# Summing the gate over partitions on VectorE instead of TensorE, in an expert MLP kernel

## What is computed

```python
x = x + (einsum('bsd,bdh->bsh', x, W[cat]) + b[cat])     # layer 0; B=2, S=1024, D=256
# layer 1, on that x:
s0   = relu(x @ swi[0]) @ swo[0]                         # shared expert 0, F=1024
s1   = relu(x @ swi[1]) @ swo[1]                         # shared expert 1
eo   = relu(x @ wi[type]) @ wo[type]                     # the chosen expert of each batch
gate_in = concatenate([eo[:, 0], s0[:, 0], s1[:, 0]])    # first token only: 3 x 256 numbers per batch
w    = softmax(relu(gate_in @ g1) @ g2)                  # g1: 768 x 256, g2: 256 x 3
out  = x + eo * w[0] + s0 * w[1] + s1 * w[2]
```

## Time and profile before

| | |
|---|---|
| median of 3 runs | 271.71 us (271.42 to 271.82) |
| the profiled execution's own time | 271.66 us |
| its span (first to last instruction) | 269.8 us |
| TensorE busy | 265.1 us, 98% of the span |
| VectorE, ScalarE, GpSimd busy | 160.9, 148.2, 160.8 us (55 to 60%) |
| granted TensorE clock | 0.999 of full |

### The profile page before, as it was taken

One profiled execution on the slowest core, in us unless ns is written; L12 is line 12 of the kernel. 1 busy time (PEld: TensorE's weight loads), 2 busy tenths in 40 slices (PEclk: granted clock), 3 DMA queues, 4 the chain that ended last, 5 costly groups with the idle time before them and its releaser, 6 DMA issues.

```text
span 269.8 us, 3491 instructions
## 1 busy us (share of the span) xinstructions
PE 265.1 (98%) x1182; PEld 220.3 (82%) x1182; DVE 160.9 (60%) x241; ACT 148.2 (55%) x257; POOL 160.8 (60%) x170
## 2 busy tenths in 40 slices
PE   8999999999999999999999999999999999999994
PEld 8788887888888888888888888888888888888884
DVE  3879958635644444654445565345566477685684
ACT  2597357665565655665655653745644555645320
POOL 0179989999948949938944724724725528524000
PEclk9999999999999999999999999999999999999999
DMA  6735322022012022102022112112012022000008
GB/s 193 247 106 155 117 78 79 7 75 79 6 74 78 6 73 78 58 24 78 2 78 78 34 46 78 33 46 79 19 61 78 2 78 75 2 0 2 0 12 299
DMA packets 7328, 18.30 MB, mean 68 GB/s; under 512 B 1168, under 2 KB 1936, under 8 KB 7312
## 3 DMA queue, kind: packets, MB, share of 16 engines
q1 hardware_dynamic: 6592, 16.92, 18.4%
q10 hardware_dynamic: 720, 1.18, 1.4%
HBM read 16.00 MB, written 2.10 MB: 67 GB/s over the span
## 4 chain that ended last, share of the span: by engine, by line
PE 96%; DMA 2%; SPq 1%; DVE 0%; issue 0%; ACT 0%; DVEq 0%
PE acc L657 48%; PE chain L657 24%; PE right L657 12%; PE left L657 7%; PE acc L674 4%; DMA w_raw<-cat_w 2%; PE corner L657 1%; SPq L222 1%; PE left L813 0%; DVE x L648 0%; ACT w_hi L352 0%; PE left L819 0%; SPq L224 0%; DVEq L647 0%
## 5 line engine op out<-in xcount | busy, mean ns | idle before, releaser
L264 POOL TENSOR_TENSOR m_lo<-staged,m_hi 128x512 fp32r<-128x512 f32 (+1 forms) x48 | 81.5, 1706 | 80.5 <-ACT m_hi L340 65.7
L657 PE MATMUL acc<-h_hi,m_hi 128*128 128x512 f32 x190 | 73.9, 389 | 0.0
L657 PE MATMUL acc<-h_hi,m_lo 128*128 128x512 f32 x190 | 73.9, 389 | 0.0
L657 PE MATMUL acc<-h_lo,m_hi 128*128 128x512 f32 x190 | 73.9, 389 | 0.0
L364 ACT COPY kept<-chain 128x512 f32<-128x512 f32 x66 | 38.8, 588 | 57.8 <-PE chain L657 57.8
L657 PEld LDWEIGHTS acc<-h_hi,m_lo 128*128 128x128 f32 x190 | 35.7, 188 | 7.4
L657 PEld LDWEIGHTS acc<-h_hi,m_hi 128*128 128x128 f32 x190 | 35.7, 188 | 7.4
L657 PEld LDWEIGHTS acc<-h_lo,m_hi 128*128 128x128 f32 x190 | 35.7, 188 | 7.4
L471 DVE SCALAR_TENSOR_TENSOR h_lo<-left,h_hi 128x512 fp32r<-128x512 f32 x24 | 16.6, 692 | 29.9 <-ACT h_hi L376 29.9
L264 POOL TENSOR_TENSOR staged<-staged 128x128 f32<-128x128 f32 x66 | 30.9, 482 | 1.7
L476 DVE TENSOR_TENSOR left<-left,kept 128x512 f32<-128x512 f32 x22 | 15.3, 698 | 26.7 <-PE left L657 26.7
(11 more groups left out here) (107 smaller groups left out, 442.7 us busy)
## 6 DMA issues: line engine op xcount, KB each, us to landing
staged<-mlp_w SPq DMA_DIRECT2D x22, 512.0 KB, 3.3
x<-x_t ACTq DMA_DIRECT2D x4, 256.0 KB, 3.9
staged<-mlp_w SPq DMA_DIRECT2D x4, 256.0 KB, 3.3
x<-x_t SPq DMA_DIRECT2D x4, 256.0 KB, 5.4
out_t<-x SPq DMA_DIRECT2D x2, 512.0 KB, 3.3
g_sb<-g SPq DMA_DIRECT2D x1, 768.0 KB, 3.8
out_t<-x SPq DMA_DIRECT2D x3, 256.0 KB, 3.0
w_raw<-cat_w SPq DMA_DIRECT2D x4, 128.0 KB, 3.1
```

The costliest lines, as they stand in the source:

```text
L264: return nc.gpsimd.tensor_tensor(out, a, b, ALU.subtract)
L657: last = nc.tensor.matmul(out[:, columns], half[:, slot, at:at + P], moving[:, columns], start=(start and n == 0), stop=(stop and n == 2), ...
```

## The change

The sum over the partitions of `gate_part` moves from TensorE to VectorE. The 128x512 tile is transposed in blocks of 32x32; the 32 numbers of each row of a block are then summed, which leaves 16 partial sums on each partition (partition 32 i + c holds those of quarter i, for the features that are c modulo 32). Four copies bring the four quarters side by side on partitions 0 to 31, a second row sum adds them, and relu, the product with `g2` and a row sum over 8 features per logit follow on 32 partitions. The last matmul then sums over 32 partitions instead of 128. `g2` is loaded in another layout, by two DMAs instead of one, and `PAD` grows from 40 to 152.

```diff
-PAD = 40
+PAD = 152
-        g2_sb = sb("g2_sb", [P, DC, 3])
+        g2_sb = sb("g2_sb", [SQ, DC, P // SQ, 3])          # SQ = 32
-        gate_h = sb("gate_h", [P, B * DC])
-        logit_half = sb("logit_half", [P, B, 3])
-        logit_part = sb("logit_part", [P, B, 3])
+        gate_blocks = sb("gate_blocks", [P, B * D])
+        gate_quarter = sb("gate_quarter", [P, B * D // SQ])
+        gate_all = sb("gate_all", [SQ, P // SQ, B * D // SQ])
+        gate_h = sb("gate_h", [SQ, B * D // SQ])
+        logit_terms = sb("logit_terms", [SQ, B, 3, D // SQ])
+        logit_part = sb("logit_part", [SQ, B, 3])
...
-                    sp.dma_start(g2_sb[:], g2).then_inc(g_loaded, 16)
+                    for d in range(DC):
+                        sp.dma_start(g2_sb[:, d, :, :], g2[:, d, :].rearrange("(a c) k -> c a k", c=SQ)).then_inc(g_loaded, 16)
...
+            def gate_transpose():
+
+                dve.wait_ge(gate_sums, 12)
+                nc.vector.transpose(gate_blocks[:], gate_part[:].rearrange("p b n -> p (b n)")).then_inc(gate_steps, 1)
+
+            def gate_quarters():
+                dve.wait_ge(gate_steps, 1)
+                nc.vector.tensor_reduce(gate_quarter[:], gate_blocks[:].rearrange("p (n k) -> p n k", k=SQ), AX.X, ALU.add
+                                        ).then_inc(gate_steps, 1)
+
             def gate_logits():
-                dve.wait_ge(gate_hidden_done, 1)
-                nc.vector.tensor_scalar(gate_h[:], left[:, 0:B * DC], 0.0, None, ALU.max).then_inc(gate_steps, 1)
-                dve.wait_ge(gate_steps, 1)
+                dve.wait_ge(gate_steps, 2)
+                for i in range(P // SQ):
+                    nc.vector.tensor_copy(gate_all[:, i, :], gate_quarter[i * SQ:(i + 1) * SQ, :]).then_inc(gate_steps, 1)
+                dve.wait_ge(gate_steps, 2 + P // SQ)
+                nc.vector.tensor_reduce(gate_h[:], gate_all[:].rearrange("c i n -> c n i"), AX.X, ALU.add).then_inc(gate_steps, 1)
+                dve.wait_ge(gate_steps, 3 + P // SQ)
                 for b in range(B):
...
+                    h = gate_h[:, b * (D // SQ):(b + 1) * (D // SQ)].unsqueeze(1).to_broadcast([SQ, 3, D // SQ])
+                    nc.vector.scalar_tensor_tensor(out=logit_terms[:, b, :, :], in0=h, scalar=0.0,
+                                                   in1=g2_sb[:].rearrange("c d a k -> c k (d a)"),
+                                                   op0=ALU.max, op1=ALU.mult).then_inc(gate_steps, 1)
+                dve.wait_ge(gate_steps, 3 + P // SQ + B)
+                nc.vector.tensor_reduce(logit_part[:], logit_terms[:], AX.X, ALU.add).then_inc(gate_steps, 1)
...
                 hidden_lo(j, 0)
+                if j == KEPT * GROUPS + 2:
+                    gate_transpose()
+                if j == KEPT * GROUPS + 3:
+                    gate_logits()
...
                 if j == KEPT * GROUPS + 2:
-                    gate_logits()
+                    gate_quarters()
...
-                if j == KEPT * GROUPS + 2:
+                if j == KEPT * GROUPS + 3:
 
                     pe.wait_ge(h_split, 4 * j + NTH[0])
-                    pe.wait_ge(gate_sums, 12)
-                    for b in range(B):
-                        for d in range(DC):
-                            last = nc.tensor.matmul(left[:, b * DC + d:b * DC + d + 1], gate_part[:, b, d * P:(d + 1) * P],
-                                                    ones[:, 0:1], start=True, stop=True)
-                    last.then_inc(gate_hidden_done, 1)
-                if j == KEPT * GROUPS + 3:
-                    pe.wait_ge(h_split, 4 * j + NTH[0])
-                    pe.wait_ge(gate_steps, 1 + 2 * B)
-                    nc.tensor.matmul(left[:, 8:8 + B * 3], ones[:], logit_part[:].rearrange("p b k -> p (b k)"),
+                    pe.wait_ge(gate_steps, 4 + P // SQ + B)
+                    nc.tensor.matmul(left[:, 8:8 + B * 3], ones[0:SQ, :], logit_part[:].rearrange("p b k -> p (b k)"),
                                      start=True, stop=True).then_inc(logits_done, 1)
```

More of the change, by code:

```diff
@@ L20 @@
 SLOTS = 3
+SQ = 32
 RAW_A21, RAW_S = 896, 1024
@@ L148, in build @@
         gate_sums = sem("gate_sums")
-        gate_hidden_done = sem("gate_hidden_done")
         gate_steps = sem("gate_steps")
@@ L490, in gate_partial @@
                         if kind == 0 and d == 0:
-                            dve.wait_ge(g_loaded, 32)
+                            dve.wait_ge(g_loaded, 16 * (1 + DC))
                             nc.vector.tensor_scalar(gate_part[:, b, :], row, first_token, None, ALU.mult).then_inc(gate_sums, 1)
@@ L500, in _ @@
             gate_count = [0]
-            def gate_logits():
-                dve.wait_ge(gate_hidden_done, 1)
-                nc.vector.tensor_scalar(gate_h[:], left[:, 0:B * DC], 0.0, None, ALU.max).then_inc(gate_steps, 1)
-                dve.wait_ge(gate_steps, 1)
-                for b in range(B):
-                    nc.vector.tensor_scalar(logit_half[:, b, :], g2_sb[:, 0, :], gate_h[:, b * DC:b * DC + 1], None,
-                                            ALU.mult).then_inc(gate_steps, 1)
-                for b in range(B):
[L510 to L513, removed]
+            def gate_transpose():
+                dve.wait_ge(gate_sums, 12)
+                nc.vector.transpose(gate_blocks[:], gate_part[:].rearrange("p b n -> p (b n)")).then_inc(gate_steps, 1)
@@ L718, in product @@
                 if n == 2:
-                    if j == KEPT * GROUPS + 3:
-                        pe.wait_ge(gate_steps, 1)
                     if j == KEPT * GROUPS + 4:
```

## The result

The changed kernel takes 274.49 us (median of 7, 272.69 to 274.59) against 271.71 before (271.42 to 271.82): ratio 1.0078, 95% interval 1.0062 to 1.0095. It is slower by about 0.8%, where 271.1 was forecast. Its executions fall into two bunches, three at 272.7 to 273.0 and four at 274.5; the four have a mean granted TensorE clock of 0.992 to 0.994, the three 1.000. The profiled execution is of the second kind: 274.59 us, span 272.7.

The account below looks back on a forecast made before the run. The prediction took TensorE, without a gap from the first group on, to bound the kernel. Its terms summed as 271.66 - 0.90 + 0.31 + 0.03 = 271.1 us, range 270.7 to 271.7.

Parts of the forecast that it names:

- term 1: Group 18: the gate's matmuls removed from TensorE shorten the kernel by 0.90 us.
- The transpose: VectorE, group 18, between the split of `left` and the `corner` add: 0.69 us, hidden; bounds 0 to 0.1, taken 0.
- The bound of 1.34: Slowest 128x512 VectorE instruction, in us; a transpose that slow would make a weight load in group 18 0.12 us late.
- The row sum at the end of group 18: VectorE, 512 elements, about 0.7 us, in place of five small instructions; costs nothing.
- the second DMA of `g2`: One more issue on SyncE near 30 us, whose 22 later loads wait for GpSimd anyway; costs nothing.
- The buffers' place: Buffers behind `fill` move by about 3 KB; costs nothing.
- Term 2: Group 19: eight small VectorE instructions take 1.55 us, so TensorE's logit matmul waits +0.31 us; bounds 0 to 0.69.
- the 11.2: Sign: group 19 lasting over 11.2 us, where about 10.8 was expected, would mean a wrong mechanism.
- The rule on partitions: Group 19's copies: input in another 32-partition group starts only after all earlier instructions finish; wait 0.31 us with it, 0.16 without.
- The slower rival: Group 19: TensorE waits for the gate's chain; 0.2% slower from 0.34 us for each of eight instructions: 272.3, chance 0.07.
- The logit matmul: Group 19, TensorE: over 32 partitions it keeps its two loads of 128 columns, so its 0.26 us stay.
- Term 3: Behind the logit matmul, VectorE falling behind TensorE in group 19 is paid in group 20: +0.03 us, bounds 0 to 0.15.

Follow-up runs that it names:

- the filled wait: The changed kernel with nine 512-column matmuls added on TensorE ahead of its wait for the logits: 273.15 us.
- the row-sum copies: The changed kernel with its four 32x16 copies replaced by four row sums over an axis of one element: 271.62 us, ratio 0.9992.

## Why the prediction was wrong

- *What bounds the kernel, and term 1 (-0.90)*: right. Group 18 went from 11.10 to 10.20.
- *The transpose*: right, 0.70 us, hidden; the `corner` add still idles 0.30 before it. The Trainium skill's page "Vector Engine (DVE) Microarchitecture Reference", section "3.8 The reshape front-end and per-opcode configuration", states one element per cycle and lane for it; the trace agrees, 0.70 us beside the 0.69 of other instructions of 512 elements. The bound of 1.34 that I took as the slowest instruction was a mean of four: the slowest of them took 1.77 us.
- *The row sum at the end of group 18, the second DMA of `g2`*: right, nothing. The buffers' place was not tested by itself; the groups beside 18 and 19 kept their lengths (10.20 us from group 4 on).
- *Term 2, the eight small instructions (+0.31 forecast)*: this is the step that failed. "Four copies of 16 elements, 0.16 each" were priced from rows in which GpSimd was idle or the instruction read from PSUM. In group 19 GpSimd runs from 211.06 to 216.34 without a gap, and the copies took 2.51 us and not 0.76. The chain was 3.38 and not 1.55, so TensorE's wait was 1.9. Group 19, with 14.29 us, passed the 11.2 that I had named as a sign of a wrong mechanism. The upper bound, 0.69, was wrong for the same reason: it took the slowest small row, of a moment with nothing beside it. A sign of the cause stood in the rows that I had quoted: four 128x512 subtractions of VectorE took 1339 ns in the mean, where most instructions of that size take 0.69 us. I used the 1339 as a bound for the transpose and did not ask what ran beside them; GpSimd ran there without a gap, from 29.75 to 36.7. The same line of the kernel before has one shape at both prices (least, median and most ns; the 0.69 at 4.53 and 5.59 us, ahead of GpSimd's first instruction, the long ones between 22.1 and 25.6, beside it):

```profile
L458 DVE TENSOR_TENSOR x_lo<-x,x_hi x6: 685/693/1776, 4.5 to 23.8; 128x512 fp32r<-128x512 f32 x6
```

- *The rule on partitions* that I weighed there (the Trainium skill's page "VectorE: DVE Perf Modes", section "Two Vector instructions with no wait between them"): the trace agrees. Moves that change partitions start 0.18 to 0.20 us apart when GpSimd is not in their way (0.71 and 0.75 us for four), two that don't 0.08. But it was the lesser rule. The Trainium skill's page "SBUF — State Buffer", section "Who interferes with whom", says that a VectorE copy that uses both of the engine's port pairs and a GpSimd instruction block each other, for the whole of the one that was issued first; that a VectorE instruction with two SBUF inputs contends with a GpSimd instruction that reads SBUF; and that a row sum never contends. The runs agree in all three: copies 1.26, two inputs 1.26, row sum 0.16 at the same place. It spoke against this change, and the prediction did not use it.
- *The slower rival* had the right mechanism and the right point (waiting is the chain's length less 1.24 us: 3.38 gives 2.1; the profile shows 1.9, and the logit matmul starts 2.05 after it was due), at a chance of 0.07. Its condition, 0.34 us for each of the eight, was passed in the mean, 3.38 / 8 = 0.42, and 2.51 of the 3.38 lay in four copies.
- *The clock* was in no case of mine. Behind the wait the granted clock was 0.54 for 3.4 us; it fell in 4 of the changed kernel's 7 executions, for 1.6 us more. The Trainium skill's page "TensorE: Matmul & The Clock Gate", in its Part 1 on the HAM clock gate, says that a gate sets TensorE's clock by how busy the engine has been; the filled wait, without a fall in five executions, agrees.
- *The logit matmul "keeps its 0.26"*: wrong by 0.28. Its weight load of 32 rows starts 0.32 us after the matmul ahead began and not with it; group 19 lasts 10.74 us where nothing waits, and 10.44 with 128 rows again.
- *Term 3 (+0.03)*: not contradicted. Group 20 lasted 10.20, but behind a longer wait and a lower clock than the term was worked out for; with the row-sum copies, where TensorE waited 0.4 us, it lasted 10.26, and 10.22 where nothing waited.

The profiled difference adds up: -0.90 (matmuls gone) + 1.9 (wait) + 0.3 (32 rows) + 1.6 (clock) = +2.9, measured 2.93. Without the fall of the clock it is 1.3, and the three executions at the full clock are 1.0 to 1.3 above before. So the failed price of the copies alone turned the forecast gain into a loss, through the wait; the clock and the 32 rows, which the sum did not have, made the loss larger.

## What to carry to other kernels

Price a small VectorE instruction by what GpSimd does at the moment where it will stand, not by its size: here a copy or a two-input instruction on SBUF data waited for the running GpSimd instruction, so put it where GpSimd is idle or write it with a single input and no copy. Where one shape has two durations in a trace, find out what ran beside the long one before using either. And when work leaves the engine that bounds the kernel, the work that replaces it must be ready before it is needed: the same instructions 4.7 us earlier made +0.8% into -0.25%.

## What was not expected of the hardware

- A wait of TensorE can cost more than itself: 1.9 us cost 1.6 more in 4 of 8 executions, 3.0 us cost more in 5 of 5, 0.4 us in none of 11.
- A matmul over 32 rows between matmuls over 128 costs 0.28 us more than one over 128 rows (group 19 of 10.74 against 10.44 to 10.46, in kernels with and without the change).
- One VectorE instruction more, 247 and not 246, went with a last write of 2.9 to 3.0 us and not 2.2 to 2.4, with a load of instructions at its end; why is not shown.
